# Two interleaved streams of a 12-layer decoder on one core: the fixed turn orders of all five engines are replaced by newly searched ones

## What is computed

```python
x = _layernorm(x + _L0_attn_ref(x, ...))     # L0a  attention in a linear form
x = _layernorm(x + _L0_xattn_ref(x, ctx))    # L0x  softmax, 16 heads, own and context keys
x = _layernorm(x + _L0_ffn_ref(x, ...))      # L0f  8 experts + a shared one, silu
x = _layernorm(x + _L1_attn_ref(x, ...))     # L1a  recurrent linear attention
x = _layernorm(x + _L1_xattn_ref(x, ctx))    # L1x  softmax, 16 heads of 64
x = _layernorm(x + _L1_ffn_ref(x, ...))      # L1f  8 experts, gelu
x = _layernorm(x + _L2_attn_ref(x, ...))     # L2a  feature maps, two inner norms
x = _layernorm(x + _L2_xattn_ref(x, ctx, ctx))  # L2x softmax, 16 heads of 8
x = _layernorm(x + _L2_ffn_ref(x, ...))      # L2f  8 experts + a shared one, silu
x = _layernorm(x + _L3_attn_ref(x, ...))     # L3a  causal softmax
x = _layernorm(x + _L3_xattn_ref(x, ctx, ctx))  # L3x gated retrieval, 8 heads
x = _layernorm(x + _L3_ffn_ref(x, ...))      # last: one quantised product over all
```

## Time and profile before

| | us |
|---|---|
| median of 3 runs | 1140.05 |
| lowest and highest | 1136.43, 1142.04 |
| the profiled execution, its own time | 1138.05 |
| span of the profiled execution | 1136.2 |
| PE busy | 979.7 (86%) |
| DVE busy | 570.7 (50%) |
| ACT busy | 414.3 (36%) |
| POOL busy | 44.5 (4%) |
| mean granted clock of TensorE | 0.891 |

### The profile page before, as it was taken

How to read it: one execution, slowest core, us unless ns; L and a number is a source line. 1 busy time by engine, 2 the same in 40 slices (tenths; PEclk the granted TensorE clock), 3 DMA queues, 4 the chain that set the end, 5 groups by cost and what they waited for, 6 DMA issues and landing times. The chain is left out here.

```text
span 1136.2 us, 20415 instructions
## 1 busy us (share of the span) xinstructions
PE 979.7 (86%) x8329; PEld 710.0 (62%) x8329; DVE 570.7 (50%) x1585; ACT 414.3 (36%) x873; POOL 44.5 (4%) x68
## 2 busy tenths in 40 slices
PE   7689898999899879988697979999989898898781
PEld 4237776788787846745245757868878685674431
DVE  5733567452464653634624853655346464534326
ACT  2035323243545725623024234234354463331211
POOL 1200000000100000000000000001010000000000
PEclk9699999899999979959659999989999989997755
DMA  9000003000003011110000000121000300000000
GB/s 335 10 1 2 1 1 149 2 34 1 17 1 126 1 37 39 62 73 1 1 10 1 1 1 2 56 94 34 1 17 1 126 1 1 1 1 1 1 0 19
DMA packets 6830, 35.97 MB, mean 32 GB/s; under 512 B 722, under 2 KB 4306, under 8 KB 5459
## 3 DMA queue, kind: packets, MB, share of 16 engines
q1 hardware_dynamic: 6738, 34.68, 8.2%
HBM read 34.15 MB, written 0.52 MB: 31 GB/s over the span
## 5 line engine op out<-in xcount | busy, mean ns | idle before, releaser
L641 PE MATMUL bank<-xT,weights_F 128*128 128x256 f32 x832 | 203.4, 390 | 0.7 <-ACT p L1766 0.6
L641 PEld LDWEIGHTS bank<-xT,weights_F 128*128 128x128 f32 x832 | 155.1, 196 | 21.7 <-issue 1.7
L649 PEld LDWEIGHTS bank<-weights_F,p 128*128 128x128 f32 x1088 | 134.4, 192 | 18.4 <-issue 6.5
L649 PE MATMUL bank<-weights_F,p 128*128 128x128 f32 x1088 | 140.5, 277 | 2.5 <-DVE p L1322 2.5
L1694 ACT ACTIVATE p<-bank 128x512 f32<-128x512 f32 x160 | 84.3, 602 | 137.8 <-PE bank L487 119.0
L1306 DVE SCALAR_TENSOR_TENSOR res<-bank,comb,res 128x128 f32<-128x128 f32 x184 | 55.8, 345 | 68.6 <-PE bank L649 65.1
L1322 DVE TENSOR_TENSOR p<-p,bank 128x512 f32<-128x512 f32 x72 | 49.4, 686 | 65.1 <-PE bank L641 33.1
L1147 DVE TENSOR_REDUCE m_wide<-bank 128x4 f32<-128x512 f32 x96 | 60.7, 683 | 39.3 <-PE bank L748 32.5
L1766 ACT ACTIVATE p<-bank 128x512 f32<-128x512 f32 x72 | 42.5, 597 | 96.8 <-PE bank L641 96.3
L1842 ACT ACTIVATE p<-bank 128x512 f32<-128x512 f32 x64 | 36.8, 598 | 58.4 <-PE bank L641 58.3
L513 PE MATMUL bank<-p,vz 128*32 128x128 f32 x1280 | 44.2, 286 | 9.4 <-ACT p L1694 8.8
(11 more groups left out here) (323 smaller groups left out, 1524.9 us busy)
## 6 DMA issues: line engine op xcount, KB each, us to landing
weights_F<-in_L1f SPq DMA_DIRECT2D x2, 4096.0 KB, 13.2
weights_F<-in_L0f SPq DMA_DIRECT2D x2, 3456.0 KB, 12.9
weights_F<-in_L2f SPq DMA_DIRECT2D x2, 3456.0 KB, 12.1
weights_Y<-in_L1x_kv SPq DMA_DIRECT2D x2, 1024.0 KB, 10.1
weights_Z<-in_L1x SPq DMA_DIRECT2D x2, 1024.0 KB, 11.1
weights_Y<-in_L2a SPq DMA_DIRECT2D x2, 898.0 KB, 4.4
weights_Z<-in_L2x SPq DMA_DIRECT2D x2, 449.0 KB, 3.2
weights_L3m<-in_L3m SPq DMA_DIRECT2D x2, 288.0 KB, 5.8
```

Source lines behind the costliest of these rows:

```text
L641: m = mm(b[:, k * NT:(k + 1) * NT], W[weight][:, f:f + P], s.xT[:], start=True, stop=True)
L649: m = mm(b[:, tk(u)], h[:, tk(u)], w, start=k == 0, stop=k == len(chunks) - 1)
```

## The change

Only the five strings of `TURN_ORDER` differ (and three more lines, so that later lines move by 3: L434 of before is L437 of after). Every engine still executes the same steps of each stream in the same order within the stream; what differs is where the steps of the one stand among those of the other. The diff, cut:

```diff
 TURN_ORDER = {
     "pe":
-        "a1 b1 a1 b1 a3 b1 a2 b2 a2 b2 a2 b2 a2 b1 a2 b1 a1 b2 a1 b1 a1 b2 a2 b1 a1 b1 a2 b1 a4 b1 a17 b1 a1 b2 "
...
+        "a2 b1 a1 b1 a1 b1 a1 b2 a2 b2 a4 b2 a1 b1 a4 b1 a1 b2 a1 b1 a1 b2 a1 b1 a1 b1 a2 b1 a3 b1 a12 b1 a2 b2 "
...
     "pool":
-        "a1 b1 a2 b2 a2 b2 a1 b1 a4 b1 a1 b2 a1 b2 a1 b1 a2 b1 a4 b6 a3 b3 a4 b1 a1 b2 a1 b2 a1 b2 a3 b3 ",
+        "a1 b1 a1 b2 a2 b1 a2 b1 a1 b1 a2 b1 a2 b2 a1 b2 a1 b1 a3 b1 a3 b4 a1 b2 a1 b1 a1 b1 a1 b1 a2 b1 a2 b2 a1 "
+        "b2 a1 b1 a2 b1 a1 b3 ",
     "sp":
-        "a3 b3 a18 b18 a23 b23 ",
+        "a3 b6 a18 b12 a23 b26 ",
 }
```

## The result

The changed kernel takes 1095.71 us, the median of four executions (1094.56 to 1100.41); the kernel before takes 1139.72 us beside it. The ratio is 0.962, with a 95% interval of 0.9595 to 0.9645: 43 us, or 3.8%, faster.

A forecast was written before the change was run, and what follows sets the result against it. PE bounds the kernel: its work at full clock, 141 us of waits, and the half clock's addition. Terms -5 -5 +5 -1 -2 sum to -8 us, hence 1130, or 1132 us as median; range 1116 to 1151.

The forecast's parts named there:

- place 2: L3x of a, first turn, 482.4 to 506.3: shorter half clock, 5 us gained, bounds 0 and 7.
- handover: Place 1, L0x beside L3x, 506.3 to 605.0: fewer PE waits, net 5 us gained; bounds 9 gained, 2 lost.
- places 1 to 3: The handover, a's first-turn L3x, and the end of the layers: 5 gained, 5 gained and 5 us lost.
- I take nothing for that stretch: L0x beside L3x, 547.3 to 595.1: half clock stays despite busy PE, so no clock gain counted.
- End of the layers, +5: Place 3, 955.0 to 1072.9: b further back, new PE waits uncovered, 5 us lost; bounds 0 and 11.
- Everywhere else, -1: Small covers in the rest: some 12 us of waits gone, 11 new; 1 gained, bounds 7 gained, 6 lost.
- Waits from DVE's and ACT's order, -2, bounds +8 and -10: Some 25 to 30 us of PE waits from other engines' order: 2 us gained; bounds 10 gained, 8 lost.
- Clock outside place 1 and 2, 0: Rest of the kernel: the forecast's sum held no term for the clock there.
- The clock comes back at the handover: Rival, chance 0.06: most of the 47.8 us half-clock stretch returns to full clock, 17 us more gained, 1115.
- Slower: Rival, chance 0.20: uncovered waits and half clock at b's end, plus missed tight covers, outweigh gains: 1147.
- Nothing moves: Rival, chance 0.32: gains and losses are of one size, time within 0.5%, for example 1137.
- The test that it named: Forecast wrong if half-clock share changes over 15 us either way, or PE newly waits for DVE elsewhere.

The follow-up runs named there:

- piece 3: Trace stretch from a in L3a, b ending L2x, to second-turn L0f/L0x; its new orders alone in the kernel before: 1129.89 us, ratio 0.992.
- gaps_dense: Kernel before with 33 unread 128-row matmuls filling four PE waits at the start of L0x beside L3x: 1129.78 us, ratio 0.991.
- gaps_thin: Kernel before with 33 unread matmuls on 8 rows filling four PE waits at the start of L0x beside L3x: 1146.30 us, ratio 1.006.
- piece 4: Trace stretch from second-turn L0f/L0x to b's last L3x gates; new orders from there to the kernel's end alone: 1132.91 us, ratio 0.9935.
- second_pe: Kernel before with the new order on TensorE alone from 366 to 430 us, DVE and ACT keeping theirs: 1147.07 us, ratio 1.007.
- piece 2: Trace stretch 366 to 430 us of the kernel before; all engines' new orders there alone: 1123.04 us, ratio 0.986.
- Pieces 1, 2 and 4: Three of the trace stretches; the first runs to about 366 us, and its new orders alone in the kernel before gave 1129.54 us, ratio 0.992.
- waits_dense: Kernel before with 13 unread 128-row matmuls filling two PE waits between 366 and 430 us: 1136.02 us, ratio 0.995.

## Why the prediction was wrong

- **What bounds the kernel.** Right: PE's work, its waits and the half clock; all of the gain is in the last two. The forecast wrote that down and then made its sum of waits almost alone. Two steps failed, and the bullets below give each its number: the clock, priced at 5 us (place 2) and taken at nothing at the handover and everywhere else, gave 28.7; and the waits outside places 1 to 3, put at 3 us gained, gave 16.2.
- **Handover and place 2, -5 and -5.** The sum was right (-9.7 in the trace, -9.1 by itself), the parts were not. The waits of L0x beside L3x did fall; the one behind the first L0x scores is 0.48 us instead of 2.91. But new ones came, of 3.31 us at the turned x (480.80) and 2.65 before b's L0x scores (601.26), so that piece 3 as a whole waits 1.7 us less, not 5 (the 2.44 at L516 stood in the kernel before as 2.33):

```profile
480.80 1.46 PE L437 MATMUL bank<-weights_con,x_tok 128*128 128x128 f32 x4 [3.31 <-DVE x_tok L1113]
...
530.13 0.30 PE L475 MATMUL bank<-weights_con,m_wide 128*128 128x128 f32 x1 [0.48 <-DVE m_wide L1163]
...
574.83 3.43 PE L516 MATMUL bank<-p,vz 128*32 128x128 f32 x64 [2.44 <-ACT p L1697]
...
601.26 1.02 PE L482 MATMUL bank<-neg_causal_bf,ident_bf 128*128 128x512 bf16 x4 [2.65 <-DVE mx L1158]
```

  Place 2 gave about as much as it cost. Its half clock is 17.0 us (448.8 to 455.6 and 459.1 to 469.3) instead of 23.9, so some 3.5 us came back instead of 5, and the new wait of 3.31 us follows it. So nearly all of piece 3's gain is the handover's.

  The clock gave 8.0 us in all of piece 3. The step that failed is "I take nothing for that stretch". It was drawn from one row, PE busy 40.7 of 47.8 us at 0.50. The row shows that busy was not enough there. It does not show that nothing would be. The new order sets b's L3a scores with their masks of 128 rows and 512 columns among a's L0x, and the fillers of `gaps_dense` are such matmuls. That these scores are what does it in the new order was not tested by itself. The Trainium skill, page "TensorE: Matmul & The Clock Gate", section "What's actually happening", says that the default is throttled and that activity releases it. `gaps_dense` agrees (full clock over 547 to 567.2). `gaps_thin` doesn't if activity means a busy engine (53.7 of 54.6 us busy, clock 0.50), and there the measurement decides.
- **End of the layers, +5.** The waits came as forecast. Over the last 685 matmuls ahead of b's last gates PE waits 12.0 us in the kernel before and 17.4 in the changed one, 5.4 more, and the stretch is 4.9 us longer (the kernel before first):

```profile
975.00:1075.00 100.00, 88.00 (x685) 55.71 (x681) 43.74 (x124) 32.87 (x77) 1.37 (x4) 0.87 0.00 1
928.90:1033.80 104.90, 87.50 (x685) 57.66 (x681) 43.36 (x128) 36.48 (x83) 1.37 (x4) 0.86 0.00 1
```

  The turned x of b's last L2f waits 3.06 us (2.5 forecast), the first scores behind b's L3a maxima 3.98 (1.1), the second 1.86 (1.8), and the projection, L451 before, 1.21 (1.2); the maxima themselves waited 0.55 (1.1):

```profile
974.82 0.66 PE L437 MATMUL bank<-weights_con,x_tok 128*128 128x128 f32 x2 [3.06 <-DVE x_tok L1113]
...
1012.40 3.47 PE L951 MATMUL bank<-wide,qk 64*128 64x512 f32 x8 [3.98 <-DVE m_diag L1168]
...
1020.14 1.99 PE L951 MATMUL bank<-wide,qk 64*128 64x512 f32 x8 [1.86 <-ACT p L1697]
...
1029.84 0.68 PE L454 MATMUL bank<-weights_L3a,attnT 128*128 128x128 f32 x4 [1.21 <-DVE attnT L1174]
```

  The lone L3x is the same 43.30 us. This term was right in place and size. It is hidden in piece 4 by what comes before it.
- **Everywhere else, -1.** Mis-sized together with the next term. Outside piece 3 and the end the waits fell by 5.0 + 4.9 + 6.3 = 16.2 us (the 6.3 are piece 4's 0.9 and the 5.4 that the end took). The forecast had 3 for both terms.
- **Waits from DVE's and ACT's order, -2, bounds +8 and -10.** This is the step that failed for the waits. The forecast saw that 25 to 30 us hang on the other engines' order. Then it took 2, less than a tenth of that, since it could only count covers in TensorE's. `second_pe` shows, for piece 2, what such a count is worth: TensorE's new order with the old ones around it is 8 us slower, while with the other engines' new orders it gains. How the 16.2 us divide between the engines in the other pieces isn't shown.
- **Clock outside place 1 and 2, 0.** Not in the sum at all. Pieces 1, 2 and 4 have 20.7 us of it. The forecast listed the two long stretches and the end, and not the some twenty short ones. `waits_dense` shows for two of them, in piece 2, that they follow waits, and so go with them; the one at 199.1 stands behind none of over half a microsecond. For the others it stays open what took them away.
- **The rivals.** "The clock comes back at the handover" had the mechanism, at 0.06, and a price of 17 us; the clock of all of piece 3 gave 8. "Slower" had its end and lost to gains that it didn't count. "Nothing moves" rested on the waits balancing, and they didn't. No rival priced the clock of the whole kernel. The test that it named did fire: half-clock time fell by 66 us (250 to 184 in the records), where 15 was the limit. PE's total waits came to 128.5, just under the 130 to 140 that it named.

The range failed for the same reason. Its bounds were those of the terms, and the largest term, clock in the rest of the kernel, had no bounds.

## What to carry to other kernels

Where PE is the bound and its clock moves, the clock is a term of its own, with its own bounds. Here it gave 28.7 us beside 12.5 us of waits. In one stretch it was shown that a wait is paid twice, by its length and by the slow clock behind it; at the handover the clock gave 8 us with under 2 us of waits. Look at the shapes, not at how busy PE is: matmuls on 8 rows helped the clock no more than idle time. Wide matmuls that nobody reads, put into a wait, can pay for themselves (8 us at the end of this kernel). But put between narrow ones on a busy path they cost more than they gave (1.8 us). And an order on several engines is one thing. Judge it by the answer times that all of them give together, not by the bound engine's row alone.

## What the runs showed of the hardware

- Fillers on 8 rows left the clock at 0.50 with PE busy 98% of 54.6 us. The same on 128 rows kept it at 1.00 for 47.7 us with PE busy 86%.
- With 32 more table loads on ACT (1283 ns each, 41 us of ACT, which is then busy 42% of the span) the kernel was still 43 us faster. The Trainium skill, page "ScalarE: Activation LUTs", section "What ACT_TABLE_LOAD costs", gives the same 1283 ns for a load; the trace agrees.
- With 12.5 us of waits gone, PE's busy time fell by 28.6 us for the same 8329 matmuls; 28.1 of it is half of the busy time that left the half clock (199.9 to 143.7 us).
- One order gave 47.8 us of half clock at the handover in the traces of eight kernels and 27 in both traces of a ninth. A clock stretch of a few tens of us isn't a function of the order next to it alone.
